# Pixel attention on one core: row maxima from a third of the operand, in pairs of banks

## What is computed

```python
xn = group_norm(x2, gn_scale, gn_bias)
qkv = jnp.einsum('oc,bct->bot', w_qkv, xn) + b_qkv[None, :, None]
qkv = qkv.reshape(B * N_HEADS, 3 * ch, T)
...
weight = jnp.einsum('bct,bcs->bts', q * scale, k * scale)
weight = jax.nn.softmax(weight.astype(jnp.float32), axis=-1).astype(weight.dtype)
a = jnp.einsum('bts,bcs->bct', weight, v)
```

## Time and profile before

| | us |
|---|---|
| runs | 2241.42, 2227.41, 2224.96 (median 2227.41) |
| the profiled execution | 2227.61 |
| its span, first to last instruction | 2225.8 |
| PE busy | 1979.0 (89%) |
| DVE busy | 1531.2 (69%) |
| ACT busy | 827.0 (37%) |
| POOL busy | 1029.1 (46%) |
| granted TensorE clock, mean | 0.935 of 2.4 GHz |

### The profile page before, as it was taken

The page is one execution under the profiler, slowest core; times in us unless marked ns, Lnnn a source line. Parts: engine busy times, 40 slices in busy tenths (PEclk is TensorE's granted clock), DMA queues, the critical chain, the costliest instruction groups (busy, mean ns, idle before and its releaser), DMA issues.

```text
span 2225.8 us, 36373 instructions
## 1 busy us (share of the span) xinstructions
PE 1979.0 (89%) x12212; PEld 1015.5 (46%) x12212; DVE 1531.2 (69%) x2315; ACT 827.0 (37%) x1546; POOL 1029.1 (46%) x437
## 2 busy tenths in 40 slices
PE   6999685799999999999999999999999969888885
PEld 2443232354554554544544544545544335445442
DVE  6766647787666777676777766777666127888786
ACT  0152310004544544443544443544545613333320
POOL 0243210005455355454454444454444608788787
PEclk8799888789999999999999999999999979999996
DMA  7200020232330330330330330330331020122211
GB/s 219 58 2 1 1 85 27 57 115 62 77 77 20 78 79 21 77 79 20 77 79 20 77 79 20 77 79 20 78 77 39 2 97 25 63 65 66 79 46 60
DMA packets 89664, 132.53 MB, mean 60 GB/s; under 512 B 58180, under 2 KB 58486, under 8 KB 89462
## 3 DMA queue, kind: packets, MB, share of 16 engines
q1 hardware_dynamic: 79958, 129.36, 21.1%
q10 hardware_dynamic: 9504, 0.59, 0.3%
HBM read 44.83 MB, written 25.17 MB: 31 GB/s over the span
## 4 chain that ended last, share of the span: by engine, by line
PE 71%; DVE 16%; issue 4%; DMA 4%; ACT 2%; SPq 2%; POOL 1%; POOLq 0%; DVEq 0%; ACTq 0%
PE AV L650 11%; PE S L637 11%; PE RB L621 11%; PE S L621 5%; PE SUM L660 4%; PE RB L689 4%; PE RB L885 3%; DVE MX L1276 3%; SPq L443 2%; PE AV L898 2%; PE RB L766 2%; DVE ENC L1617 2%; DVE DEV L1316 2%; PE RB L706 2%; PE RB L934 1%
## 5 line engine op out<-in xcount | busy, mean ns | idle before, releaser
L1276 DVE TENSOR_REDUCE MX<-RB 128x1 f32<-128x512 f32 x783 | 515.2, 684 | 89.3 <-PE RB L621 80.7
L1014 ACT ACTIVATE PR<-S 128x512 f32<-128x512 f32 x640 | 356.5, 597 | 578.3 <-PE S L637 559.0
L1175 POOL TENSOR_TENSOR ACC<-PR 128x1024 f32<-128x1024 f32 x72 | 170.3, 2373 | 760.6 <-ACT PR L1014 758.7
L637 PE MATMUL S<-QS,KS 98*128 98x512 f32 x1152 | 470.2, 460 | 17.4 <-issue 8.5
L1175 POOL TENSOR_TENSOR ACC<-ACC,PR 128x1024 f32<-128x1024 f32 x152 | 360.0, 2371 | 198.2 <-ACT PR L1014 189.4
L621 PE MATMUL RB<-KS,QS 96*128 96x512 f32 x783 | 393.1, 524 | 32.7 <-DVE MX L1276 20.1
L1014 ACT ACTIVATE X<-S 128x512 f32<-128x512 f32 x512 | 283.7, 597 | 284.0 <-PE S L637 277.2
L621 PEld LDWEIGHTS RB<-KS,QS 96*128 96x128 f32 x783 | 245.0, 318 | 251.6 <-DVE MX L1276 153.0
L637 PEld LDWEIGHTS S<-QS,KS 98*128 98x128 f32 x1152 | 222.4, 198 | 218.5 <-issue 93.6
L1276 DVE TENSOR_REDUCE MX<-S 128x1 f32<-128x512 f32 x369 | 251.7, 682 | 32.2 <-PE S L621 27.0
L621 PE MATMUL S<-KS,QS 96*128 96x512 f32 x369 | 186.3, 505 | 11.4 <-DVE MX L1276 6.8
(11 more groups left out here) (235 smaller groups left out, 2096.3 us busy)
## 6 DMA issues: line engine op xcount, KB each, us to landing
X<-out_y SPq DMA_DIRECT2D x24, 1024.0 KB, 5.1
QS<-HI SPq DMA_DIRECT2D x144, 128.0 KB, 2.4
KS<-HI SPq DMA_DIRECT2D x144, 128.0 KB, 2.5
out_y<-X SPq DMA_DIRECT2D x16, 1024.0 KB, 4.1
QS<-LO SPq DMA_DIRECT2D x72, 128.0 KB, 2.6
KS<-LO SPq DMA_DIRECT2D x72, 128.0 KB, 2.4
X<-in_x SPq DMA_DIRECT2D x8, 1024.0 KB, 8.7
OHU<-out_y SPq DMA_DIRECT2D x8, 512.0 KB, 4.4
```

The costliest lines, as they stand in the source:

```text
L637: mm(ST[:, (H * s + h) % BANKS, :], KS[par][:, h, P * mt:P * mt + P], QS[par][:, h, HALF * half:HALF * half + HALF], start=True, stop=True ...
L1014: nc.scalar.activation(exps(i, s, pair)[:, HALF * one:HALF * one + HALF], ST[:, (H * s + h) % BANKS, :], ACT.Exp, scale=1.0 if i is None e ...
L1175: nc.gpsimd.tensor_tensor(ACC[:, pair, :], so_far, exps(i, s, pair), ALU.add).then_inc(pool_used, 1)
L1276: nc.vector.tensor_reduce(out=MX[:, h, t, half:half + 1], in_=bank(), op=ALU.max, axis=AX.X).then_inc(ring_free, 1)
```

## The change

The diff, cut to its core. `maxima(jobs)` and `others(jobs)` select the "max" jobs of a step and the rest.

```diff
-BANKS = 3
+BANKS = 2
+RING_BANKS = (0, 1, 2, 3)
...
+    def take(self, width=1):
+        first = self.at + -self.at % width
+        self.at = (first + width) % len(self.banks)
+        places = [self.banks[(first + n) % len(self.banks)] for n in range(width)]
+        self.prior = max(self.user.get(p, 0) for p in places)
+        self.k += 1
+        self.user.update((p, self.k) for p in places)
+        return places[0]
...
+QUADS = [(t, half) for t in range(MT) for half in range(2)]
+QUAD_STEPS = (1, 2, 3, 4, 4, 5, 6, 7, 8, 8, 9, 10, 11, 12, 13, 14)
...
     if nxt:
-        tiles = [("max", h, t, half) for h in range(H) for t in range(MT) for half in range(2)]
-        load = [sum(DVE_SHARE[j[0]] for j in step) for step in jobs]
-        steps = range(1, STEPS)
-        room = min(r for r in range(200)
-                   if sum(max(0, r - load[s]) // DVE_SHARE["max"] for s in steps) >= len(tiles))
-        for s in steps:
-            n = max(0, room - load[s]) // DVE_SHARE["max"]
-            jobs[s] += tiles[:n]
-            tiles = tiles[n:]
-        assert not tiles
+        for s, (t, half) in zip(QUAD_STEPS, QUADS):
+            jobs[s] += [("max", hp, t, half) for hp in range(2)]
...
+for _n, _extra in enumerate(([("v", 1)], [("qk", 0, 0)], [("qk", 0, 1), ("qk", 1, 0)], [("qk", 1, 1)])):
+    START += [("max", _hp, _t, _half) for _t, _half in QUADS[4 * _n:4 * _n + 4] for _hp in range(2)]
+    START += _extra
...
-        ST = S4[:, 0:BANKS, :]
-        RING = [S4[:, BANKS, :], RB[:, 0, :], RB[:, 1, :]]
+        ST = RB
         FRONT = RB[:, 0, :]
+        def ring_bank(place, width=1):
+            if place >= len(RING_BANKS):
+                return RB[:, place - len(RING_BANKS), :]
+            return S4[:, place, :] if width == 1 else S4[:, place:place + width, :]
...
-                        load(QS[par][D * j:D * j + D, h, :].bitcast(f32), q[rows, 0, :].bitcast(f32), stk[h])
-                        load(KS[par][D * j:D * j + D, h, :].bitcast(f32), k[rows, 1, :].bitcast(f32), stk[h])
+                        to = D * ((h + j) % 3)
+                        load(QS[par][to:to + D, h, :].bitcast(f32), q[rows, 0, :].bitcast(f32), stk[h])
+                        load(KS[par][to:to + D, h, :].bitcast(f32), k[rows, 1, :].bitcast(f32), stk[h])
...
-                    wait(sp, negmax_ready, H * u + h + 1)
+                    wait(sp, negmax_ready, 2 * u + h // 2 + 1)
...
+            def bank(width=1):
+                place = ring.take(width)
+                if ring.prior:
+                    wait(pe, ring_free, ring.base + ring.prior)
+                return ring_bank(place, width)
...
-            def max_scores(u, par, h, t, half):
-                if t == 0 and half == 0:
-                    wait(pe, stk[h], 96 * (u + 1))
-                mm(bank(), QS[par][0:3 * D, h, t:N:MT], KS[par][0:3 * D, h, HALF * half:HALF * half + HALF],
-                   start=True, stop=True).then_inc(ring_full, 1)
+            def max_scores(u, par, hp, t, half):
+                dst = bank(2)
+                for n in range(2):
+                    h = 2 * hp + n
+                    if t == 0 and half == 0:
+                        wait(pe, stk[h], 96 * (u + 1))
+                    row = slice(D * (h % 3), D * (h % 3) + D)
+                    last = mm(dst[:, n, :], QS[par][row, h, t:N:MT],
+                              KS[par][row, h, HALF * half:HALF * half + HALF], start=True, stop=True)
+                last.then_inc(ring_full, 1)
...
-                    scores(u, par, s, (0,))
-                    run(jobs[s][0:1])
-                    scores(u, par, s, (1, 2))
-                    run(jobs[s][1:3])
+                    scores(u, par, s, (0, 1))
+                    run(maxima(jobs[s]))
+                    scores(u, par, s, (2, 3))
+                    run(others(jobs[s]))
                     if s:
                         values(u, par, s - 1, i)
+                        sums(u, s - 1, i)
                     elif trail:
                         values(u - 1, 1 - par, STEPS - 1, i)
-                    run(jobs[s][3:4])
-                    scores(u, par, s, (3,))
-                    run(jobs[s][4:5])
-                    if s:
-                        sums(u, s - 1, i)
-                    elif trail:
                         sums(u - 1, STEPS - 1, i)
-                    run(jobs[s][5:])
...
-            def row_max(u, par, h, t, half):
-                nc.vector.tensor_reduce(out=MX[:, h, t, half:half + 1], in_=bank(), op=ALU.max,
+            def row_max(u, par, hp, t, half):
+                two = slice(2 * hp, 2 * hp + 2)
+                nc.vector.tensor_reduce(out=MX[:, two, t, half], in_=bank(2), op=ALU.max,
                                         axis=AX.X).then_inc(ring_free, 1)
                 if t == MT - 1 and half == 1:
                     own()
-                    wait(dve, rows_in[h], 2 * 16 * u)
-                    link(nc.vector.tensor_reduce(out=NM[:, h, :], in_=MX[:, h], op=ALU.max, axis=AX.X,
+                    for h in (2 * hp, 2 * hp + 1):
+                        wait(dve, rows_in[h], 2 * 16 * u)
+                    link(nc.vector.tensor_reduce(out=NM[:, two, :], in_=MX[:, two], op=ALU.max, axis=AX.X,
                                                  negate=True))
-                    link(nc.vector.tensor_copy(NMH[:, h, :], NM[:, h, :]))
-                    nc.vector.tensor_tensor(NML[:, h, :], NM[:, h, :], NMH[:, h, :].bitcast(f32),
+                    link(nc.vector.tensor_copy(NMH[:, two, :], NM[:, two, :]))
+                    nc.vector.tensor_tensor(NML[:, two, :], NM[:, two, :], NMH[:, two, :].bitcast(f32),
                                             ALU.subtract).then_inc(negmax_ready, 1)
...
-                    run(jobs[s][0:3])
+                    run(maxima(jobs[s]))
                     if s == (1 if par == 1 and i is None else INVERT_AT) and trail:
                         invert(2 * u - 1)
                     if s == MT + INVERT_AT:
                         invert(2 * u)
-                    run(jobs[s][3:])
+                    run(others(jobs[s]))
```

More of the change, by code:

```diff
@@ L51, with __init__ @@
 class Tally:
-    def __init__(self, banks=BANKS):
-        self.base, self.k, self.banks, self.first = 0, 0, banks, 0
+    def __init__(self):
+        self.base, self.k = 0, 0
     def add(self, n=1):
@@ L149, with maxima, others @@
 START = []
-for _h in range(H):
-    START += [("max", _h, _t, _half) for _t in range(MT) for _half in range(2)]
-    START += [[("v", 1)], [("qk", 0, 0)], [("qk", 0, 1), ("qk", 1, 0)], [("qk", 1, 1)]][_h]
+for _n, _extra in enumerate(([("v", 1)], [("qk", 0, 0)], [("qk", 0, 1), ("qk", 1, 0)], [("qk", 1, 1)])):
+    START += [("max", _hp, _t, _half) for _t, _half in QUADS[4 * _n:4 * _n + 4] for _hp in range(2)]
+    START += _extra
+def maxima(jobs):
+    return [job for job in jobs if job[0] == "max"]
+def others(jobs):
+    return [job for job in jobs if job[0] != "max"]
 def after_jobs():
@@ L165, in first_jobs @@
 def first_jobs():
-    maxima = [("max", h, t, half) for h in range(H) for t in range(MT) for half in range(2)]
+    maxima = [("max", hp, t, half) for t, half in QUADS for hp in range(2)]
     jobs = {("concepts", 1): [("stats",)], ("softmax", 1): [("gn", 0)], ("turn", 1): [("gn", 1)],
@@ L586, in _ @@
         def _(pe):
[L587 removed]
+            ring = Ring(RING_BANKS)
             pe_need = Tally()
             mm = nc.tensor.matmul
[L591 to L594 removed]
+            def bank(width=1):
[3 more added lines that the diff above has]
+                return ring_bank(place, width)
             def all_read():
@@ L1223, in _ @@
         def _(dve):
-            ring = Tally()
+            ring = Ring(RING_BANKS)
             steps = Tally()
@@ L1234, in link, with bank @@
                     dve.wait_ge(dve_step, steps.add())
-            def bank():
-                wait(dve, ring_full, ring.add())
-                return RING[ring.slot()]
+            def bank(width=1):
+                place = ring.take(width)
+                wait(dve, ring_full, ring.now())
+                return ring_bank(place, width)
             def own():
```

35 lines of the change are left out of this document (19 added, 16 removed).

## The result

| | before | after |
|---|---|---|
| median of the runs | 2228.15 us (4 runs, 2224.96 to 2241.42) | 2654.21 us (4 runs, 2634.9 to 2673.09) |
| ratio | | 1.191 [1.182, 1.200] |
| the profiled execution, its span | 2227.61, 2225.8 us | 2650.77, 2648.9 us |
| granted clock, mean | 0.935 | 0.850 |

What follows compares the result with a forecast made beforehand. PE's list was taken to set the time, so any stop of PE is paid in full. Stack wait 205, steps 60, clock 32 and the rest 17 sum to 314 us on 2227.6: 2540 us, range 2380 to 2680.

Steps and rivals of the forecast that it cites:

- Part 1: Step 1 of each of 16 windows: PE waits for all four heads' stacks, 12.8 us a window, +205 us.
- rival D: The stack wait is smaller, some 6 us, because transfers are issued faster with PE and DVE still: 2320 us, chance 0.04.
- a wait of under 9 us a window: Sign against the prediction: PE's wait for the stacks stays below 9 us in each window.
- Part 2: The windows' steps apart from the stack wait: +6 us in each odd window, +2 in each even one, +60 us.
- the change of shape: Maxima in 32 rows change the array's shape: 0.45 us in and out, 6.3 us over 14 steps of a window.
- steps 4 and 8: Four pairs share two places there, so later pairs wait for reductions: 5.4 us a window, steps near 7 and 8 us.
- two score banks: Head 2's scores wait for head 0's exponential; pairs cover this except in step 15: 1.5 us with head 3.
- Part 3: Low clock behind the new stall: 2 us in each of 16 windows, +32 us.
- Part 4: The rest: +7 us ahead of window 0, +9 in window 17, +5 in window 1, -4 in second-unit maxima; +17 us.
- A: The wait alone costs: changing rows causes no drain, steps 4 and 8 hide in DVE's slack, clock holds; 2385 us, chance 0.20.
- B: Pairs do not run side by side, each matmul of a quad has its own weight load: 2665 us, chance 0.11.
- C: Faster: half the matmul work for maxima, less shape changing by `sums`, and the wait does not bind; 2115 us, chance 0.03.

Runs made afterwards that it cites:

- e4: The kernel before with each unit's first maximum waiting for the stacks of all four heads instead of head 0's: 2436.49 us, 1.092.
- e2: The changed kernel with the eight HI.HI transfers of a unit issued first under their own semaphores, the maxima waiting for those alone: 2482.1 us, 1.112.
- e1: The changed kernel with all pairs of heads 0 and 1 first, then those of heads 2 and 3, at the same steps: 2509.81 us, 1.124.
- r11: The changed kernel with 96-partition maxima, heads 0 and 1's pairs first, pairs in steps 2 to 15 (at most three), old transfers: 2388.91 us, 1.073.
- r12: The kernel before with two score banks in place of three, its ring, order and maxima kept: 2300.68 us, 1.030.
- e3: The changed kernel with eight and six float32 filler matmuls ahead of the waits for head 2's and head 3's stacks: 2738.44 us, 1.227.
- e7: The kernel before with its maxima made from 32 partitions (the leading halves) in place of 96, nothing in pairs: 2736.22 us, 1.229.
- r10: The changed kernel with its maxima made from all 96 partitions again, pairs, banks, steps and waits kept: 2581.75 us, 1.159.
- e6: The changed kernel with the leading halves of all four heads at partitions 0 to 31, undoing the three row places: 2724.26 us, 1.224.
- e9: The kernel before with `sums` right behind `values` in a step and head 3's scores behind both: 2279.78 us, 1.024.

## Why the prediction was right, and where its sum was off

**Sign and mechanism.** The forecast's case is the one that came: the wait for the stacks in step 1 (e4 puts it in for +208 us, e2 and e1 take out 172 and 144), steps slower rather than faster, a clock that falls in every window.

**Part 1, the wait, as forecast in steps 0 and 1, with other pieces.** The last stack transfer landed 18.4 us after window 7's start, not 21.6. SP starts 1.4 us into the window instead of 3.0, and its 24 transfers take 14.6 us from first to last instead of 16.3, 0.64 us each. Part 1 had said that nothing lets SP start sooner and had kept its pace; that is the direction of rival D, by 3 of its 6 us. D's reason is not shown, since r11, which has no such stall, has 14.6 us in its odd windows from 5 on as well; but the pace is not the fixed one that was held against D. PE also came late, 9.9 us into the window and not 8.2. So it stood still for 6.5 us instead of 12 to 13.

Of the 142.4 us in the table of waits, 14.1 stand ahead of window 0 and 2.2 in window 1; the other 126 are 7.9 us a window where Part 1 had 12.8. The prediction had named a wait of under 9 us a window as a sign of being wrong, and that sign came: the case is right, the size of its main term is not. But step 0 and all behind the wait ran at 1.2 GHz in part, and the two steps together are 13.4 us longer (odd) and 17.1 us (even). e4's 12.7 us a window stands near Part 1's 12.8, but it holds 10.8 us of waiting, in the old order and at SP's old start, and the clock behind it. That the total came within 114 us is in part luck: some 80 us too much in Part 1 stand against the terms below, which were too small.

**Part 2, the steps, mis-sized.** Right: the change of shape (0.50 us measured, 0.45 taken), the places that run side by side, the odd windows' steps 2, 6 and 14 (3.2 to 3.5 us, forecast 3.5). Too small: steps 4 and 8, forecast near 7 and 8 us and measured at 9.1 and 9.2 in window 7. The 4 us that even windows were to get back from DVE did not show: their steps 2 to 15 are 9.6 us longer in window 6. The clump in the timeline:

```profile
1107.59 1.24 PE L660 MATMUL S<-KS,QS 32*128 32x512 f32 x4
...
1109.73 0.82 PE L660 MATMUL S<-KS,QS 32*128 32x512 f32 x2 [0.90 <-DVE MX L1312]
...
1110.86 0.81 PE L660 MATMUL S<-KS,QS 32*128 32x512 f32 x2 [0.32 <-DVE MX L1312]
...
1111.61 1.22 PE L677 MATMUL RB<-QS,KS 98*128 98x512 f32 x2
...
1112.76 1.94 PE L690 MATMUL AV<-X,VT 128*32 128x512 f32 x8
```

The waits for the reduction are there as described, and every matmul around them runs at 1.2 GHz (1.22 and 1.94 us against 0.73 and 1.07); `values` of step 3 (1104.58, 1.93 us) already does, so the clock had fallen ahead of the clump. Left out: two score banks were costed at 1.5 us a window because the pairs cover them. Head 2 is covered by two pairs, which take 0.80 us and not the 1.5 of the text; steps 9 to 12 grew by 0.6 to 1.1 us each, and r12 shows 4 us a window even in the old order.

**Part 3, the clock, the term that failed most.** 2 us a window were taken from one idle stretch. Window 7 spends 27 us at 1.2 GHz where it had none. Pairs of rows at either level give a price: v product and `values` of step 0 2.87 + 1.74 against 1.95 + 1.07 us, the scores, v product and `values` of step 1 1.22 + 3.62 + 1.31 against 0.73 + 1.95 + 1.07, and some 1 us in step 3, 2 in step 4 and 1 in step 8. That is an estimate of 8 us a window, 128 us for 16, worked out from rows of window 7, of e3 and of before; the even windows 4 to 14 have 37 to 41 us at 1.2 GHz, so it is rather low. It overlaps with the steps' excess above, so the two must not be added. The step of the argument that failed is that only the new stall would lower the clock. The wait alone (e4) brings 14 us of 1.2 GHz into window 7 and, with all that comes with it, some 2.5 us a window, near Part 3's 2. The 32-row maxima alone (e7) bring 46 us with PE never idle; the change without its stall (e2) has 10 us left, the change without its 32-row matmuls (r10) 17. r10 shows 72 us of the change's time to hang on those matmuls.

**Part 4** gave +7 ahead of window 0, +9 in window 17 and, in the stretch of window 1, +5 and -4; measured are +9.1, +12.3 and +10.2 us. The -8.4 us behind window 17 is no effect of the change: in e4, whose code there is that of before, that stretch is as short (454.3 us against 462.6 in before's profiled execution).

**The rivals.** A (changing rows costs nothing) falls by e7's 0.98 us. B came nearest in time (2665) and is wrong in its cause: three places do start together, and e6, which is B, costs 70 us more. So its nearness is luck. The Trainium skill's section that was cited for it (TensorE: Matmul & The Clock Gate, Part 3, The mechanism) says that a weight load overlaps only in another row group, and also names a background weight buffer as a way around that. The first is not what these rows show: in r10 the four 96-row maxima of a quad share all their row groups and still take 0.98 us, 0.24 us each, less than the 0.31 us of a weight load. C did not come.

**What stays open.** The loss of window 7, +25.5 us, can be told by stretches, but its causes lean on one another (a stall lowers the clock, the clock lengthens a clump), so no sum of single terms is shown. Of r11's 164 us, 67 are the banks if they cost there what they cost in the old order. In the profiled executions r11 stands 85 us above r12: 70 in the 16 windows and 12 ahead of window 0, where it still waits for all four heads' stacks. For the windows' part the traces name the step's order with two banks and step 0's wait for rows, and no run separates them. The change with three score banks and single ring banks wasn't tried, nor the new order of a step alone.

## What to carry to other kernels

When a list of jobs that went head by head is interleaved over heads, look when each head's operand lands: the old order may have been hiding the transfers, and the first interleaved job waits for the last of them with everything behind it. Fewer rows in a matmul of the same columns save nothing by themselves; among work of another shape they cost the way in and out (0.50 us here) and can cost the clock. When a change adds stalls or small shapes to an engine that bounds the kernel, price the work around them at the lower clock too, and count how many scores a bank holds up before taking a bank away.

## What the runs showed of the hardware

- Three 32-row matmuls in different row places start within 40 ns; a fourth in a place already taken starts 0.47 us after the first (timeline of window 7, 1102.22 to 1102.70). A quad is 0.80 us in three places, 1.29 in one, and 0.98 in the 96-row shape.
- The granted clock of a PE that the profile shows as never idle fell when its maxima had 32 rows in place of 96: 0.79 in a window that had 1.00 (e7).
- Small operations of DVE took two microseconds beside POOL's additions. In the kernel before (window 6, step 4) and in e9 (window 6, step 5), by the timelines:

```profile
835.44 1.95 DVE L1284 CAST NMH<-NM 128x8 fp32r<-128x8 f32 x1
837.43 0.17 DVE L1285 TENSOR_TENSOR NML<-NM,NMH 128x8 fp32r<-128x8 f32 x1
```

```profile
850.74 4.66 POOL L1172 TENSOR_TENSOR ACC<-ACC,PR 128x1024 f32<-128x1024 f32 x2 [1.25 <-ACT PR L1011]
...
850.99 0.17 DVE L1279 TENSOR_REDUCE NM<-MX 128x8 f32<-128x16 f32 x1
851.19 1.94 DVE L1281 CAST NMH<-NM 128x8 fp32r<-128x8 f32 x1
...
853.17 2.26 DVE L1282 TENSOR_TENSOR NML<-NM,NMH 128x8 fp32r<-128x8 f32 x1
...
856.08 0.31 PEld L621 LDWEIGHTS RB<-KS,QS 96*128 96x128 f32 x1 [4.15 <-DVE MX L1273]
```

In e9 the copy and the subtraction of 8 elements a partition take 1.94 and 2.26 us while POOL runs two additions, each ending about where one of POOL's does (2.33 us each), and PE then waits 4.15 us for a ring bank. In the kernel before the copy takes as long beside one addition, and the subtraction behind it 0.17 us. So what e9's order adds is the second addition right behind the first and the long subtraction: 14 of 72 subtractions take over 1 us, none before. Why DVE is held there was not tested.
